# Graph attention kernel: VectorE's pieces of a chunk's weights in five sub-batches, scalings and sums one sub-batch later, a ring of 23 places

## The reference

```python
Q = (einsum('nc,rch->rnh', x, Wq) + bq[:, None, :]).reshape(R, N, HEADS, OUT)   # K, V alike
q_i, k_j, v_j = Q[edge_type, dst], K[edge_type, src], V[edge_type, src]
score = sum(q_i * k_j, axis=-1) * scale
seg = dst * R + edge_type
m = segment_max(score, seg);  e = exp(score - m[seg]);  s = segment_sum(e, seg)
out = segment_sum(v_j * (e / s[seg])[..., None], dst)
x = layernorm(x + out.reshape(N, 256) + bias)
```

## Time and profile before

| | |
|---|---|
| median of 3 runs | 2039.41 us (2039.25 to 2039.56) |
| the profiled execution's own time, its span | 2043.67 us, 2041.9 us |
| busy over the span | PE 83%, DVE 79%, ACT 51%, POOL 56% |
| edge loop, first to last `products` | 790.1 to 1889.6 us |
| from the last `products` to the end of the sums | to about 1960 us |
| chain that ended last | DVE 35%, PE 33%, issue 16%, POOL 8% |
| DMA | 555 MB, 272 GB/s over the span |

### The profile page before, as it was taken

One profiled execution on the slowest core, in us unless ns is written; L12 is line 12 of the kernel. 1 busy time (PEld: TensorE's weight loads), 2 busy tenths in 40 slices (PEclk: granted clock), 3 DMA queues, 4 the chain that ended last, 5 costly groups with the idle time before them and its releaser, 6 DMA issues.

```text
span 2041.9 us, 33205 instructions
## 1 busy us (share of the span) xinstructions
PE 1692.2 (83%) x7565; PEld 1136.7 (56%) x7565; DVE 1619.3 (79%) x4151; ACT 1045.8 (51%) x4107; POOL 1152.7 (56%) x1215
## 2 busy tenths in 40 slices
PE   5999999999999995687788877788777887788645
PEld 2444444444444443466666666666666676677534
DVE  7988897454443344799999999999999999999548
ACT  1223330200000000378888788788888888878835
POOL 2000005777777505777777777777777777776105
PEclk9999999999999997899999999999999999989668
DMA  6333344999999948999999999999999999998006
GB/s 214 124 124 109 124 141 160 313 350 364 364 362 363 339 154 292 339 318 329 320 316 320 318 333 311 320 320 321 334 309 321 320 326 329 324 306 291 24 22 210
DMA packets 339496, 555.34 MB, mean 272 GB/s; under 512 B 44045, under 2 KB 238831, under 8 KB 339298
## 3 DMA queue, kind: packets, MB, share of 16 engines
q0 software_dynamic: 80880, 256.60, 36.7%
q1 hardware_dynamic: 222180, 228.67, 34.2%
q10 hardware_dynamic: 36238, 67.94, 9.2%
HBM read 412.09 MB, written 140.94 MB: 271 GB/s over the span
## 4 chain that ended last, share of the span: by engine, by line
DVE 35%; PE 33%; issue 16%; POOL 8%; DMA 4%; DVEq 2%; ACT 1%; SPq 0%; ACTq 0%; POOLq 0%
PE sums L633 24%; POOL region L468 8%; DVE region L996 6%; DVE region L1267 5%; DVE region L1210 4%; PE pairs L709 4%; DVE region L1199 3%; PE sums L697 3%; DMA region<-kv_tab,kvidx 3%; DVE acc L1293 3%; DVE region L1276 2%; DVEq L1284 1%; DVE region L1221 1%; DVE region L1400 1%; DVE region L1403 1%
## 5 line engine op out<-in xcount | busy, mean ns | idle before, releaser
L468 POOL DMA_INDIRECT region<-kv_tab,kvidx x831 | 818.2, 985 | 361.1 <-issue 214.8
L881 ACT ACTIVATE region<-region 128x64 f32<-128x64 f32 x2496 | 694.1, 351 | 0.0
L633 PE MATMUL sums<-region,acc 128*128 128x512 f32 (+2 forms) x1568 | 679.5, 579 | 4.1 <-DVE region L1171 3.3
L709 PE MATMUL pairs<-region 128*128 128x256 f32 x1664 | 449.4, 416 | 181.7 <-DVE region L1210 156.4
L709 PEld LDWEIGHTS pairs<-region 128*128 128x128 f32 x1664 | 323.3, 204 | 256.6 <-issue 195.1
L697 PE MATMUL sums<-region 128*128 128x131 f32 x3328 | 438.5, 286 | 28.1 <-issue 24.5
L633 PEld LDWEIGHTS sums<-region,acc 128*128 128x128 f32 (+1 forms) x1568 | 284.8, 190 | 305.9 <-issue 290.4
L697 PEld LDWEIGHTS sums<-region 128*128 128x128 f32 x3328 | 417.1, 199 | 60.2 <-issue 52.2
L1177 DVE TENSOR_TENSOR region<-sums,region 128x512 f32<-128x512 f32 (+1 forms) x245 | 168.7, 690 | 249.9 <-PE sums L633 245.5
L450 POOL DMA_INDIRECT region<-q_tab,region x288 | 275.3, 956 | 92.8 <-issue 61.3
L899 ACT COPY acc<-sums 128x256 f32 x832 | 305.9, 368 | 30.0 <-PE sums L697 28.6
(11 more groups left out here) (246 smaller groups left out, 953.0 us busy)
## 6 DMA issues: line engine op xcount, KB each, us to landing
region<-q_seg SPq DMA_DIRECT2D x832, 128.0 KB
kv_tab<-region ACTq DMA_DIRECT2D x48, 1280.0 KB, 7.7
q_seg<-region SPq DMA_DIRECT2D x288, 128.0 KB, 5.3
q_tab<-region SPq DMA_DIRECT2D x48, 640.0 KB, 3.3
region<-rel_tab SPq DMA_DIRECT2D x208, 128.0 KB, 5.2
region<-kv_tab,kvidx POOLq DMA_INDIRECT x831
region<-in_x SPq DMA_DIRECT2D x96, 128.0 KB, 3.1
out<-region SPq DMA_DIRECT2D x48, 128.0 KB, 2.3
```

What stands on the lines that cost most here:

```text
L468: pool.indirect_dma_start(ring_row[:, a:a + 2 * C], None, kv_tab, bass.IndirectOffsetOnAxis(ap=kvidx[:, t:t + 1], axis=0)).then_inc(s_got[ ...
L633: done = nc.tensor.matmul(bank[o % 4][0:n, 0:w], acc[:, k, t * P:t * P + n], w_sb[:, k, :, :].rearrange("p u c -> p (u c)")[:, c0:c0 + w], ...
L709: done = nc.tensor.matmul(qk[:, i, :], oht[:, s % 2, i * P:(i + 1) * P], qring[:, s % QS, i, :], start=True, stop=True)
L881: done = nc.scalar.activation(ring_v[:, i, spot(q), h * D:(h + 1) * D], ring_v[:, i, spot(q), h * D:(h + 1) * D], ACT.Copy, scale=alT[:, h ...
```

## The change

VectorE's pieces move: the scans of the exponentials from the b-slot of age 2 to the a-slot of age 3, the second `carries` from the a-slot to the b-slot of age 3, full scans, sum and difference from the b-slot of age 3 to the a-slot of age 4, reciprocal and product to the a-slot of age 5. TensorE's and ScalarE's pieces follow. Scalings and sums of a sub-batch come one step later (`AHEAD` 12 to 13, `LAG` 13 to 14), so each loop has one step more, and the ring of keys and values has 23 places instead of 22.

```diff
-    AHEAD = 12
+    AHEAD = 13
     LAG = AHEAD + 1
-    KS = 22
+    KS = 23
 # TensorE
             def weights_a(s):
                 if k == 1:
                     turn_rows(c, 0)
                 if k == 3:
-                    turn_carries(c, 1)
-                if k == 4:
-                    pe.wait_ge(s_al, c + 1)
-                    nc.tensor.transpose(bank[6][:, P:2 * P], al[:], ident[:]).then_inc(s_aT, 1)
+                    turn_rows(c, 1)
             def weights_b(s):
                 if k == 1:
                     turn_carries(c, 0)
-                if k == 2:
-                    turn_rows(c, 1)
+                if k == 3:
+                    turn_carries(c, 1)
+                if k == 5:
+                    pe.wait_ge(s_al, c + 1)
+                    nc.tensor.transpose(bank[6][:, P:2 * P], al[:], ident[:]).then_inc(s_aT, 1)
 # ScalarE
                 if k == 3:
-                    move_carries(2 * c + 2)
+                    move_rows(2 * c + 2)
...
                 if k == 1:
                     move_carries(2 * c + 1)
-                if k == 2:
-                    move_rows(2 * c + 2)
+                if k == 3:
+                    move_carries(2 * c + 2)
+            def take_weights(s):
+                if k == 6:
+                    act.wait_ge(s_aT, c + 1)
...
+                    nc.scalar.copy(alT[:], bank[6][:, P:2 * P]...).then_inc(s_alT, 1)
                 for i in range(SB):
                     if places:
                         place_window(q - 1, i, at)
+                    if i == 0:
+                        take_weights(s)
...
-                take_weights(s)
 # VectorE
             def weights_a(s):
                 if age == 3:
-                    carries(k, 1, total)
+                    dve.wait_ge(s_exp, k + 1)
+                    scans(ends, x_ex, XF[:, k, :], total, (0.0, 0.0)).then_inc(s_ends, 1)
+                if age == 4:
+                    dve.wait_ge(s_car, 2 * k + 2)
+                    c(scans(full, x_ex, XF[:, k, :], total, (car[:, 0:1], car[:, 1:2])))
+                    c(nc.vector.tensor_tensor(D_sb[:], full[:, 0, :], full[:, 1, :], ALU.add))
+                    nc.vector.tensor_tensor(D_sb[:], D_sb[:], x_ex[:], ALU.subtract).then_inc(s_D, 1)
+                if age == 5:
+                    dve.wait_ge(s_D, k + 1)
+                    c(nc.vector.reciprocal(al[:], D_sb[:]))
+                    nc.vector.tensor_tensor(al[:], al[:], x_ex[:], ALU.mult).then_inc(s_al, 1)
             def weights_b(s):
-                if age == 2:
-                    dve.wait_ge(s_exp, k + 1)
-                    scans(ends, x_ex, XF[:, k, :], total, (0.0, 0.0)).then_inc(s_ends, 1)
                 if age == 3:
-                    dve.wait_ge(s_car, 2 * k + 2)
...
-                    nc.vector.tensor_tensor(al[:], al[:], x_ex[:], ALU.mult).then_inc(s_al, 1)
+                    carries(k, 1, total)
```

More of the change, by code:

```diff
@@ L849, in weights_a @@
                 if k == 3:
-                    move_carries(2 * c + 2)
-            def take_weights(s):
-                c, k = piece(s)
+                    move_rows(2 * c + 2)
                 if k == 4:
@@ L856, in take_weights @@
                     nc.scalar.copy(recD[:, :, c], D_sb[:, 0:P:P - 1])
[L857 to L862, removed]
             def weights_b(s):
@@ L870, in weights_b @@
                     move_carries(2 * c + 1)
-                if k == 2:
-                    move_rows(2 * c + 2)
+                if k == 3:
+                    move_carries(2 * c + 2)
+            def take_weights(s):
+                c, k = piece(s)
+                if k == 6:
+                    act.wait_ge(s_aT, c + 1)
+                    if c > 0:
+                        act.wait_ge(s_pay, ACT_TILES * PERC * c)
+                        act.wait_ge(s_pay_dve, PERC * c)
+                    nc.scalar.copy(alT[:], bank[6][:, P:2 * P].rearrange("p (h g) -> p h g", h=H)).then_inc(s_alT, 1)
             def payload(q, i, pair):
```

## The result

The changed kernel takes 2019.53 us (median of 4 runs, 2016.91 to 2022.04), the kernel before 2039.33 beside it: ratio 0.9902, 95% interval 0.9887 to 0.9916. Forecast were 2016.2 in a range of 2007 to 2028, so 19.8 us were gained of the 23.2 foretold. The profiled execution took 2022.04 (span 2020.2) where the sum said 2020.5.

What follows compares the result with a forecast made beforehand. VectorE's list was taken as the bound, POOL only 3% behind. 1.2 us over 22.85 chunks saves 27.4, less 4.2 at the end: 2043.67 to 2020.5 profiled; the median, 4.26 lower, is 2016.2, range 2007 to 2028.

Steps and rivals of the forecast that it cites:

- VectorE's list sets the steps: Edge loop: VectorE, busy 96.8 of 100 us, sets the step times; its pieces lengthen a step from 4.35 to 8.17 us.
- the load's gap: VectorE's idle entry ahead of a product, where the register load stood behind another product: about 0.46 us per chunk saved.
- The slots of the moved pieces: VectorE's a- and b-slots: pieces taken out cost 4.50 us, put in 3.32, so 1.18 us saved per chunk.
- POOL caps the gain at 41.3 per chunk: POOL's gathers need 41.3 us per chunk, unchanged, only 3% from being the bound, limiting any relief of VectorE.
- VectorE alone would need 41.1: VectorE's new list per chunk: 41.49 us with its present waits for data (up to 0.4), 41.1 without.
- The clock: TensorE falls to 1.2 GHz once per chunk after waiting 3.71 us at age 3; expected to go, worth part of 0.4.
- ScalarE's copy at age 6: ScalarE's `alT` waits for TensorE's transpose: costed at nothing; as a slower rival, about 2.5 us late, 2073 us, chance 0.03.
- The added step: End of the loop: one more step behind the last product, costing 4.2 us.
- The drain rule's (2033): Rival: moved slots on VectorE bring nothing, only the register load's 0.46 us per chunk goes; 2033 us, chance 0.10.
- The ring's (2043.6): Slower rival: release of ring places sets the pace, chunk stays at 42.67 us, end pays 4.2; 2043.6 us, chance 0.09.
- That VectorE's waits would go too: Rival: VectorE's waits for late data vanish, POOL's 41.3 us per chunk becomes the pace; 2012 us, chance 0.22.

Runs made afterwards that it cites:

- e4_norec: Changed kernel without VectorE's reduction of a chunk's end columns (a memset instead, end corrections left out of the result): 2011.07 us.
- e7_add: Changed kernel with VectorE's third add of a step moved behind the reduction to scores: 2006.45 us, ratio 0.9832.
- e1_load: Kernel before, with only VectorE's register load moved to the end of the step before, ahead of the b-slot: 2031.23 us, ratio 0.9952.
- e3_fill: Kernel before with ten transposes of the identity added on TensorE at the end of its step of age 3: 2040.29 us, ratio 0.9999.
- e2_depth: Kernel before with the change's depth alone (AHEAD 13, ring of 23), ScalarE's alT copy at the end of age 5: 2037.49 us, ratio 0.9988.
- e6_four: Changed kernel with reciprocal and product at age 4 and the old depth (AHEAD 12, ring of 22): 2019.49 us, ratio 0.9893.
- the last runs: Kernel before with load and third add moved (1.0009, again 0.9965); four-sub-batch version with third add moved (0.9883, again 0.9878); the change again (0.9898).

## Why the prediction was right, point by point

- **VectorE's list sets the steps**: held, before and after. `e4_norec` shows it by taking from the list, `e7_add` by filling a gap. Where the time went, from start to start per chunk in the traces before and after: the last product of the weights to the next instruction 0.75 and 0.20 us (the load's gap), the adds 3.49 and 2.95, the difference 0.32 and 0.21 (filled gaps), together 1.20 saved; the wide masks 3.24 and 3.42, 0.18 given back; the rest is within 0.1.
- **The slots of the moved pieces.** Age 3, a-slot: 1301.21 - 1300.49 = 0.72, less 0.30, is 0.42 (0.45 foretold). Age 4: 1307.45 - 1305.96 = 1.49, less 0.30, is 1.19 (1.19). Age 5: 1.25 less 0.30 is 0.95 (1.01). The b-slot of age 3: from the masks at 1303.21 to the product at 1304.71 are 1.50, less 0.79, is 0.71 (0.67). Together 3.27 (3.32). The load's gap: 0.46 foretold, entry gone; `e1_load` measures 8.6 us for it where 10.5 were worked out, which its interval (7 to 12) does not exclude; its wide masks grew as well (512 ns on the mean, 488 before).
- **POOL caps the gain at 41.3 per chunk**: wrong. Its gathers got shorter (966 ns, so 1.271 with the gap, 40.7 us per chunk), and it still waits. I had taken 986 ns as POOL's own in the sum ("These masks stay"), though it was partly what the meeting with VectorE's masks costs, and that moves with the order of the instructions. A cap there is, but at 40.9, where `e7_add` runs into it.
- **VectorE alone would need 41.1**: not so. Its waits for late data went, as foretold, but they were 4.2 us in 21.1 chunks, 0.2 each and not 0.4, and the wide masks took 0.18 more. The two cancel, which is why the 41.45 of the forecast and the 41.44 measured agree: that closeness is luck, the saving by the slots is not. By the same starts the saving is 1.10 per chunk instead of 1.2, since the kernel before stands at 42.54 and not at 42.67; the loop gained 25.2 us instead of 27.4.
- **The clock.** I expected the drop to go. TensorE's longest wait fell to 1.9 us, but the clock still drops 9 times in 900 us (20 before), not in each chunk. It is worth little: `e3_fill` has 16 drops instead of 20 and the same time, and `e7_add`, with 15, is 13 us faster than the change with 9.
- **ScalarE's copy at age 6** cost nothing that shows: its waits for the transpose fell from 56.9 to 23.7 us, the longest from 4.3 to 1.7. **The added step**: 3.7 us against 4.2, near by luck in part. Other pairs of traces have 1.6 (`e1_load` and `e2_depth`) and 8.3 (`e6_four` and the change) behind the last product, so its price is not settled.
- **The median** is 3.3 us over the forecast, 1.6 of them in the profiled execution too; the remainder is within the spread of its runs (2016.9 to 2022.0).
- **The rivals.** The drain rule's (2033) fell with the rows of the slots and with `e7_add`. The ring's (2043.6) fell: POOL's waits for sums shrank. That VectorE's waits would go too came true, but the 0.2 us that it gave went to the masks, so the 2012 did not follow.

## What to carry to other kernels

Where one in-order engine is busy 97%, don't only add up what it does: look for instructions behind which nothing can run ahead (a register load behind a result that is waited for) and for two short dependent instructions in a row, and put independent work between them. That gave 8.6 us (`e1_load`) and 13 us (`e7_add`, on top of the change) for a few moved lines, together as much as the whole change, which holds the first of the two. In the slower condition of the last runs the two together gave almost nothing without the spreading. And when you cost a second engine that is near the bound, ask which part of its mean is contention with the first: that part moves when the order does.

## What was not expected of the hardware

The fp32 masks and the gathers disturb each other: a mask of 128x131 takes 281 ns without gathers and 311 to 321 with them, and it is the end of a gather that matters, for masks that lie between start and end take 279; a gather takes 942 ns at best and 966 to 986 on the mean. Ten transposes with the same operand overlap to 1.25 us where one alone takes 0.27. And in the last runs, on two chips, what waits for another engine often started 1 to 2 us late, for every kernel alike: the time of the kernel before rose from 2040 to 2347 us, while the ratio of the change stayed at 0.990.
